# Turned context stored by the attention and read back by the feature stage, in place of a second turn

## The chip, the core and the metric

One core of a Trainium2 chip runs the whole program in one launch. TensorE (PE) multiplies, with its weight loads shown as PEld; VectorE (DVE), ScalarE (ACT) and GpSimd (POOL) do the elementwise work; SyncE (SP) issues most transfers, POOL some. The metric is the device time of the launch in microseconds, lower is better.

## The reference, cut to what matters

Four layers run one after another on x, 16 batches of 128 rows by 512 features: attention over a context, a ternary linear layer, an attention between features, and a mixture of 16 experts. The change concerns what the first and third layers share, the context `ctx` (16 x 128 x 512):

```python
k = (memory_tokens @ wk.T); v = (memory_tokens @ wv.T)            # first layer, memory_tokens = ctx

def _L1_xattn_ref(Q, K, V):                                       # third layer, K = V = ctx
    x = jnp.einsum('bdn,bdm->bnm', Q, K) / sqrt(dk)
    score = jax.nn.sigmoid(x)
    return jnp.einsum('bvn,bnm->bvm', V, score)

x = x + jnp.tanh(g_xattn[1]) * _L1_xattn_ref(_layernorm(x, axis=-1), ctx_2048, ctx_2048)
```

For each batch the third layer forms a 512 x 512 table of scores and multiplies the context by it.

## The kernel before, in words

All matrix products keep single precision by splitting each operand into a high part (rounded by a copy to the fp32r type) and a low part (the rest), and by three matmuls: high by high, high by low, low by high. `mm3` (lines 45 to 49) issues them, so every product shows as L47, L48 and L49.

The first two layers and the third lie in `attention_and_ternary`. The order of work is written out by hand: strings of words such as `cT.2 q.1.2` are turned by `steps` into one list, `plan`, and each engine walks that list and issues its own part of every step. The strings are `start`, `first_group`, `group` (twice) and `last_group`, for four groups of four batches; behind them a loop over `m` from 0 to 63 writes the feature stage's order, four values of `m` per batch. `between` mixes in what is left of the ternary layer and the first steps of what follows.

**Attention.** Step `cT.b` turns a batch's context: PE transposes four 128 x 128 pieces into a PSUM bank (L502), ACT copies the high part into `cT`, DVE subtracts to get the low part. `cT` holds four batches (two pairs), each reused by the batch four later. The key and value products read it.

**Feature stage.** Per batch b: SP loads the context again, unturned, into one of four places (`cx.b`, L387). POOL splits it into high and low for the scores (`ks.b`: L449, L451, and L453 for the low part of the normed x; tiles of `Wk`). ACT makes the normed x and its high part (`an`, L713; `qh`, L721). PE makes four score products (`aS`, output SC). ACT takes the sigmoid twice (`ag`, L726 and L729), DVE subtracts for the low part (L869, tile `Wq`). PE makes four value products into one bank M (`ap` three times, then `aO`), whose left operand is the turned context `avT`, in the tile of `Wv`. DVE adds the result to X and takes its statistics (L874, L877).

The turned context comes from step `aT.b`: PE transposes the loaded context as in attention (L502, tile T), ACT copies the high part (L660) and DVE subtracts (L881). `avT` has two places. `aT.0` and `aT.1` stand at the end of `last_group`; `aT.{b+1}` stands before the third value product of batch b. The step also makes SP wait before it loads the batch four later into the same place:

```python
if n == 2 and 1 <= b + 1 < NB and b:
    text += [f"aT.{b + 1}"]
...
sp.wait_ge(t_fill, at(T_KINDS, ("aT", b - GB)))
sp.wait_ge(aq_lo, b - GB + 1)
```

`wait` and `wait_ge` hold an engine until a counter is reached; everything behind on that engine stands still too.

Of the kernel before, what the change touches and what calls it, by code (L numbers as in the profile page):

```python
# [114 lines left out]
def attention_and_ternary(nc, c, x, g_x, g_f, fw, fb, ctx_in, mask, norm_w, wq, wk, wv, wo, wg, sw1, sw2, sw3):  # L115

    X, identF = c["X"], c["identF"]
    with ExitStack() as st:
# [3 lines left out]
        def sem(name):  # L122
            return st.enter_context(nc.semaphore(name))
# [49 lines left out]
        avT = flat(W["v"][:, :, :, :])[:, 0:4 * D].rearrange("p (b h d) -> p b h d", b=2, h=2)  # L173
# [22 lines left out]
        TILED = ("xT", "cT", "v", "g", "S", "rc", "bc", "pv", "oT", "oP", "st", "sf", "sx", "nm", "mk", "u", "uT", "fm")  # L196

        def steps(text, g):
# [31 lines left out]
        start = ("W.k Wh.k Wl.k mf cT.0 cT.1 gt W.q Wh.q Wl.q sx.0 sx.1 sx.2 sx.3 xa.0 k.0.0 k.0.1 W.v Wh.v Wl.v.0.1 xb.0 Wl.v.2.3 "  # L230
# [33 lines left out]
        for m in range(MS):  # L264
# [8 lines left out]
            if n == 2 and 1 <= b + 1 < NB and b:  # L273
                text += [f"aT.{b + 1}"]
# [3 lines left out]
            if n == KC - 1 and b + GB < NB:  # L278
                text += [f"cx.{b + GB}"]
# [5 lines left out]
        SPLIT, T_KINDS = ("xT", "cT", "aT", "rT"), ("xT", "cT", "aT", "rT", "pT", "bc", "uT", "ft")  # L285
# [34 lines left out]
        ac_in = [sem(f"ac_in{n}") for n in range(GB)]  # L320
# [18 lines left out]
        with nc.Block() as block:  # L339
            @block.sync  # L340
            def _(sp):
# [35 lines left out]
                for s in plan:  # L377
                    if s[0] == "cx":
# [3 lines left out]
                        elif b < GB:  # L382
                            sp.wait_ge(s_fill, 4 * (NB - 2))
                        else:
                            sp.wait_ge(t_fill, at(T_KINDS, ("aT", b - GB)))
                            sp.wait_ge(aq_lo, b - GB + 1)
                        sp.dma_start(aCX[b % GB], ctx_in[b]).then_inc(ac_in[b % GB], 16)  # L387
                    elif s[0] == "rn":
# [22 lines left out]
            def _(pool):  # L411
# [20 lines left out]
                for s in plan:  # L432
# [5 lines left out]
                    elif kind == "tb":  # L438
# [3 lines left out]
                            .then_inc(a_powered, 1)  # L442
                    elif kind == "ks":
# [32 lines left out]
            def _(pe):  # L476
# [11 lines left out]
                def transposes(s, tf):  # L488
# [9 lines left out]
                    else:  # L498
                        src = {"rT": lambda k: rows[:, t, k * P:(k + 1) * P], "aT": lambda k: aCX[t % GB][:, k * P:(k + 1) * P], "xT": lambda k: xn[:, t % 2, k * P:(k + 1) * P], "cT": lambda k: CT[:, t % 2, k * P:(k + 1) * P],
# [33 lines left out]
                for s in plan:  # L533
# [8 lines left out]
                    elif kind in T_KINDS:  # L542
# [7 lines left out]
                        elif kind == "aT":  # L550
                            pe.wait_ge(ac_in[t % GB], 16 * (t // GB + 1))
# [22 lines left out]
                    elif kind in ("ap", "aO"):  # L574
                        n = s[2] if kind == "ap" else KC - 1
                        m, mf = KC * t + n, at(M_KINDS, ("aO", t))
                        if n == 0:
                            wait(pe, m_act, up_to(M_KINDS, BY_ACT, mf - 2))
                            wait(pe, m_dve, up_to(M_KINDS, BY_DVE, mf - 2))
                            pe.wait_ge(t_lo, at(SPLIT, ("aT", t)))  # L580
# [1470 lines left out]
```

## Time and profile before

| What | Value |
|---|---|
| Median of 3 runs | 1234.98 us (1234.42 to 1236.65) |
| The profiled execution | 1236.93 us |
| Its span in the trace | 1235.2 us, so 1.73 us lie around it |
| PE busy | 1162.0 us, 94% of the span |
| DVE, ACT, POOL busy | 685.9, 579.1 and 438.0 us |
| Granted TensorE clock, mean | 0.989 of full speed |
| First value product to the last update of X | 377.1 to 492.7 us |

The profile gives each engine's busy time, the time it sat idle and the instruction that ended each idle stretch. A busy PE is not PE at its peak, since matmuls overlap; where they run back to back, the distance between two starts is the price of one.
### The profile page before, as it was taken

What the parts mean: (1) busy time and instruction counts of PE and PEld (TensorE: products, weight loads), DVE (VectorE), ACT (ScalarE), POOL (GpSimd) and SP (SyncE); (2) the same over time, 40 slices, a digit from 0 to 9 for tenths busy, and PEclk for the clock granted to TensorE, in tenths of its full rate; (3) what the DMA queues carried; (4) which work ended last, traced back from release to release, by engine and by line L of the source; (5) the groups of instructions that cost most, each with busy time, mean ns of one, the idle gap of its engine ahead of it and who ended that gap; (6) DMA issues with size and microseconds to landing.
All of it is one profiled execution on the core that took longest, in us unless ns stands there. A gap on an engine that the chain in (4) does not pass through costs nothing. (4 is left out here: it accounts for less than half of the span.)

```text
span 1235.2 us, 24835 instructions
## 1 busy us (share of the span) xinstructions
PE 1162.0 (94%) x7376; PEld 995.7 (81%) x7388; DVE 685.9 (56%) x1411; ACT 579.1 (47%) x1389; POOL 438.0 (35%) x530
## 2 busy tenths in 40 slices
PE   6999999999998898799999998999999999999995
PEld 6887888887876676577777877899999989998995
DVE  6776756666559999435766545432244452424241
ACT  5665645656578697631111115433344453434342
POOL 1103212213337663100047622444444435444443
PEclk9999999999999999899999999999999999999998
DMA  9110000000001210220002316664456574646464
GB/s 334 53 38 1 19 4 18 19 21 12 25 1 36 96 44 31 91 96 1 1 1 72 138 52 206 153 152 76 77 138 145 147 208 85 142 81 144 79 142 72
DMA packets 54332, 100.31 MB, mean 81 GB/s; under 512 B 5094, under 2 KB 21990, under 8 KB 54262
## 3 DMA queue, kind: packets, MB, share of 16 engines
q0 software_dynamic: 15824, 37.76, 16.0%
q1 hardware_dynamic: 38438, 61.65, 15.1%
q8 instruction: 40, 0.66, 0.2%
q14 instruction: 30, 0.25, 0.1%
HBM read 72.91 MB, written 26.48 MB: 80 GB/s over the span
## 5 line engine op out<-in xcount | busy, mean ns | idle before, releaser
L1901 PE MATMUL t_H<-m_W,t_xT 128*128 128x352 f32 x1632 | 281.9, 328 | 6.8 <-DVE m_W L1979 5.3
L1901 PEld LDWEIGHTS t_H<-m_W,t_xT 128*128 128x128 f32 x1632 | 263.2, 189 | 10.0 <-DVE m_W L1979 7.7
L1869 POOL DMA_INDIRECT out_dram<-t_ys,t_sid x68 | 109.6, 1612 | 223.8 <-ACT t_ys L1930 117.4
L738 ACT ACTIVATE pr<-SC,neg 128x128 f32<-128x128 f32 x256 | 90.7, 377 | 57.5 <-DVE neg L948 56.2
L1946 ACT ACTIVATE t_sl<-t_H 128x352 f32<-128x352 f32 x68 | 31.6, 465 | 175.3 <-PE t_H L1901 175.3
L2024 DVE TENSOR_TENSOR t_hT<-t_TH,t_hT 128x384 fp32r<-128x384 f32 x68 | 37.8, 556 | 101.8 <-ACT t_hT L1967 100.7
L2000 DVE TENSOR_TENSOR t_h<-t_H,t_sl 128x352 f32<-128x352 f32 x68 | 35.6, 524 | 105.0 <-ACT t_sl L1946 105.0
L47 PE MATMUL t_Y<-m_W,t_hT 128*128 128x512 f32 (+1 forms) x207 | 88.0, 425 | 4.8 <-issue 3.0
L1930 ACT ACTIVATE t_ys<-t_Y,t_wcol 128x512 f32<-128x512 f32 x69 | 47.4, 687 | 94.6 <-PE t_Y L49 94.6
L49 PE MATMUL t_Y<-m_W,t_hT 128*128 128x512 f32 (+1 forms) x207 | 82.2, 397 | 0.0
L48 PE MATMUL t_Y<-m_W,t_hT 128*128 128x512 f32 (+1 forms) x207 | 81.9, 396 | 0.0
L1214 POOL TENSOR_SCALAR m_W<-m_W,bst 128x128 fp32r<-128x128 f32 x64 | 49.6, 793 | 31.6 <-PE eL L1329 31.4
L869 DVE TENSOR_TENSOR Wq<-kT,Wq 128x512 fp32r<-128x512 f32 x64 | 56.2, 903 | 6.7 <-ACT Wq L729 6.6
L1410 ACT ACTIVATE ehT<-eh 128x512 fp32r<-128x512 f32 (+1 forms) x24 | 15.2, 632 | 91.8 <-DVE eh L1696 91.8
L738 ACT ACTIVATION_READ_ACCUMULATOR pr<-SC,neg 128x1 f32 x256 | 54.9, 215 | 0.0
L945 DVE TENSOR_REDUCE mx<-SC 128x4 f32<-128x512 f32 x64 | 43.8, 685 | 18.4 <-PE SC L629 18.2
L1860 POOL COPY t_sid<-m_vals 128x1 uint32 x68 | 52.8, 776 | 0.5 <-issue 0.5
L465 POOL TENSOR_TENSOR X<-X,upd 128x512 f32<-128x512 f32 x16 | 21.3, 1330 | 88.0 <-DVE upd L929 88.0
L1861 POOL COPY m_pos<-m_rowid 128x1 uint32 x68 | 51.6, 759 | 0.0
L47 PEld LDWEIGHTS t_Y<-m_W,t_hT 128*128 128x128 f32 (+1 forms) x207 | 39.4, 190 | 13.5 <-issue 5.8
L1020 POOL DMA_INDIRECT m_first<-rows_d,m_pos x36 | 37.3, 1035 | 35.0 <-POOL m_pos L1861 26.6
L1975 DVE TENSOR_TENSOR t_xT<-t_TX,t_xT 128x512 fp32r<-128x512 f32 x69 | 47.7, 691 | 3.2 <-ACT t_xT L1923 0.3
(454 smaller groups left out, 3135.5 us busy)
## 6 DMA issues: line engine op xcount, KB each, us to landing
m_raw<-in_L_ffn_w_dram SPq DMA_DIRECT2D x28, 704.0 KB, 5.8
m_raw<-in_L_ffn_w_dram SPq DMA_DIRECT2D x14, 512.0 KB, 6.9
CT<-in_ctx_dram SPq DMA_DIRECT2D x8, 512.0 KB, 3.8
X<-in_x_dram SPq DMA_DIRECT2D x4, 1024.0 KB, 13.3
rows_d<-rows_first SPq DMA_DIRECT2D x16, 256.0 KB, 2.0
out_dram<-X SPq DMA_DIRECT2D x3, 1024.0 KB, 4.3
m_raw<-in_L_ffn_w_dram SPq DMA_DIRECT2D x14, 192.0 KB, 6.7
CT<-in_ctx_dram SPq DMA_DIRECT2D x8, 256.0 KB, 2.7
```

Of the source, the lines that this page charges most:

```text
L47: pe.matmul(out, lhs(0), rhs(0), start=first, stop=False)
L48: pe.matmul(out, lhs(0), rhs(1), start=False, stop=False)
L49: return pe.matmul(out, lhs(1), rhs(0), start=False, stop=last)
L738: i = act.activation(pr[:, t % 2, slot, :], SC[t % HQ][:, slot * S:(slot + 1) * S], ACT.Exp, scale=SCALE0, bias=neg[:, t % 2, slot:slot + ...
L869: dve.tensor_tensor(as_[:, n, 1, :], asg[:, n, :], as_[:, n, 0, :].bitcast(F32), ALU.subtract).then_inc(as_lo, 1)
L1214: i = pool.tensor_scalar(tab_a[t % SLOTS][:, k, :], iP.bitcast(F32), place_p[:, t, k:k + 1], None, ALU.is_equal)
L1860: pool.tensor_copy(sid[:, b:b + 1], m["target"][:, bass.ds(n, 1)]).then_inc(zeroed, 1)
L1861: pool.tensor_copy(gid[:, b:b + 1], rowid[:, bass.ds(n + UT, 1)]).then_inc(zeroed, 1)
L1869: pool.indirect_dma_start(out=m["out_rows"][:, :], out_offset=bass.IndirectOffsetOnAxis(ap=sid[:, b:b + 1], axis=0), in_=ys[:, b, :], in_o ...
L1901: x_ = pe.matmul(bk[b % 2][:, 0:I], xT[:, b % 2, jx, k, :], W13[:, jw, k, j, :], start=k == 0 and jx == jw, stop=k == KC - 1 and jx == 1)
L1930: act.activation(ys[:, (b - 1) % UT, :], Y[(b - 1) % 2][:, :], ACT.Copy, scale=wcol[:, (b - 1) % UT:(b - 1) % UT + 1]).then_inc(y_evac, 1)
L1975: dve.tensor_tensor(xT[:, b % 2, 1, :, :], TX[:, :].rearrange("p (k t) -> p k t", k=KC), xT[:, b % 2, 0, :, :].bitcast(F32), ALU.subtract) ...
```

## The change

The attention's turned context, high and low, is stored to a scratch tensor in DRAM, `av_d`, in 16 new steps `sv.b` on SP, each behind the low part of `cT.b`. The feature stage reads it back in 16 new steps `al.b`, issued by POOL, into four places of `avT`. The 16 steps `aT.b` go, on PE, ACT and DVE.

```diff
-        avT = flat(W["v"][:, :, :, :])[:, 0:4 * D].rearrange("p (b h d) -> p b h d", b=2, h=2)
+        avT = flat(W["v"][:, :, :, :]).rearrange("p (b h d) -> p b h d", b=GB, h=2)
+        av_d = nc.dram_tensor("av_d", [NB, P, 2, D], F32, kind="Internal").ap()
...
-            "pT.15 u.0 qh.1 aS.0.2 bc.3 pv.3 ks.1 oT.3 uT.0 aT.0 aT.1 ag.0.1 oP.3 u.1 fm.0 ")
+            "pT.15 u.0 qh.1 aS.0.2 bc.3 pv.3 ks.1 oT.3 al.0 al.1 al.2 al.3 uT.0 ag.0.1 oP.3 u.1 fm.0 ")
...
-            if n == 2 and 1 <= b + 1 < NB and b:
-                text += [f"aT.{b + 1}"]
...
             if n == KC - 1 and b + GB < NB:
-                text += [f"cx.{b + GB}"]
+                text += [f"cx.{b + GB} al.{b + GB}"]
...
                         else:
-                            sp.wait_ge(t_fill, at(T_KINDS, ("aT", b - GB)))
                             sp.wait_ge(aq_lo, b - GB + 1)
...
+                    elif s[0] == "sv":
+                        b = s[1]
+                        sp.wait_ge(t_lo, at(SPLIT, ("cT", b)))
+                        sp.dma_start(av_d[b].rearrange("p h (k t) -> p h k t", k=KC), cT[:, b // 2 % 2, :, :, b % 2 * S:(b % 2 + 1) * S].bitcast(F32))\
+                            .then_inc(av_out[b % GB], 16)
...
+                    elif kind == "al":
+                        b = t
+                        pool.wait_ge(av_out[b % GB], 16 * (b // GB + 1))
+                        if b < GB:
+                            projected(pool, "v", NB - 1)
+                        else:
+                            summed(pool, KC * (b - GB) + KC - 1)
+                        pool.dma_start(avT[:, b % GB, :, :], av_d[b].bitcast(F32R)).then_inc(av_in[b % GB], 16)
...
-                            pe.wait_ge(t_lo, at(SPLIT, ("aT", t)))
+                            pe.wait_ge(av_in[t % GB], 16 * (t // GB + 1))
...
+                            if kind == "cT":
+                                wait(act, av_out[t % GB], 16 * (t // GB))
```

`summed(pool, KC * (b - GB) + KC - 1)` waits for the last value product of batch b - 4. The words `sv.2` to `sv.5` stand in each group some steps behind the `cT` of the same number, and `al.4` to `al.15` each at the end of batch b - 4's part of the loop. The last hunk makes ACT wait, before it overwrites a place of `cT`, until the store of the batch four earlier has landed. SP has 16 more transfers in the attention, each of 1024 pieces of 128 elements; POOL has 16, of 128 x 1024 elements.

DVE at the end of batch 1 in the feature stage, before (`Wq` is the scores' tile, `Wv` the turned context's, `M` the value product's bank, `bst` the statistics):

```order
L900 BN_STATS bst<-X 128x6
L869 TENSOR_TENSOR Wq<-kT,Wq 128x512 x2
L900 BN_STATS bst<-X 128x6
L869 TENSOR_TENSOR Wq<-kT,Wq 128x512
L881 TENSOR_TENSOR Wv<-T,Wv 128x512
L869 TENSOR_TENSOR Wq<-kT,Wq 128x512
L874 SCALAR_TENSOR_TENSOR X<-M,tg,X 128x512
L877 BN_STATS bst<-X 128x6
```

and the same place with the change:

```order
L900 BN_STATS bst<-X 128x6
L874 TENSOR_TENSOR Wq<-kT,Wq 128x512 x2
L900 BN_STATS bst<-X 128x6
L874 TENSOR_TENSOR Wq<-kT,Wq 128x512 x2
L879 SCALAR_TENSOR_TENSOR X<-M,tg,X 128x512
L882 BN_STATS bst<-X 128x6
```

The subtraction for the turned context has gone from between two of the scores' low parts; nothing else moved. PE and ACT lose their part of the step in the same way.

POOL from the second key split to the fourth, before (`Wk` holds the splits, `fbrow` and `upd` are what the ternary layer adds to X):

```order
L453 TENSOR_TENSOR Wk<-xn,Wk 128x512
L469 TENSOR_TENSOR X<-X,fbrow 128x512
L465 TENSOR_TENSOR X<-X,upd 128x512
L473 TENSOR_TENSOR X<-X,upd 128x512
L449 CAST Wk<-qT 128x512
L451 TENSOR_TENSOR Wk<-qT,Wk 128x512
L453 TENSOR_TENSOR Wk<-xn,Wk 128x512
L469 TENSOR_TENSOR X<-X,fbrow 128x512
L473 TENSOR_TENSOR X<-X,upd 128x512
L449 CAST Wk<-qT 128x512
```

and with the change:

```order
L464 TENSOR_TENSOR Wk<-xn,Wk 128x512
L453 DMA Wv<-av_d 128x1024 x4
L480 TENSOR_TENSOR X<-X,fbrow 128x512
L476 TENSOR_TENSOR X<-X,upd 128x512
L484 TENSOR_TENSOR X<-X,upd 128x512
L460 CAST Wk<-qT 128x512
L462 TENSOR_TENSOR Wk<-qT,Wk 128x512
L464 TENSOR_TENSOR Wk<-xn,Wk 128x512
L480 TENSOR_TENSOR X<-X,fbrow 128x512
L453 DMA Wv<-av_d 128x1024
L484 TENSOR_TENSOR X<-X,upd 128x512
L460 CAST Wk<-qT 128x512
```

Four transfers now stand behind the second key split and one ahead of the fourth; one more follows in each later batch, up to batch 11's.

## Rows read from the trace of the kernel before

**Rows 1.** Windows: engine busy times, granted clock, DMA share; attention, then the feature stage

```profile
60.00:340.00 280.00, 269.50 (x2412) 231.06 (x2419) 187.26 (x454) 161.80 (x593) 72.29 (x67) 1.00 0.06 17
...
377.00:400.00 23.00, 19.91 (x90) 14.56 (x88) 22.55 (x37) 18.16 (x35) 19.70 (x15) 1.00 0.09 24
400.00:440.00 40.00, 34.09 (x151) 26.26 (x154) 36.53 (x53) 28.32 (x54) 25.66 (x20) 0.96 0.27 86
440.00:493.00 53.00, 47.94 (x221) 37.40 (x219) 50.26 (x83) 44.96 (x85) 26.49 (x21) 1.00 0.09 27
```

**Rows 2.** Timeline of DVE: the update of X (L874) closing a batch

```profile
384.28 0.74 DVE L874 SCALAR_TENSOR_TENSOR X<-M,tg,X 128x512 f32<-128x512 f32 x1
...
448.50 0.75 DVE L874 SCALAR_TENSOR_TENSOR X<-M,tg,X 128x512 f32<-128x512 f32 x1
...
455.18 0.74 DVE L874 SCALAR_TENSOR_TENSOR X<-M,tg,X 128x512 f32<-128x512 f32 x1
...
492.66 0.75 DVE L874 SCALAR_TENSOR_TENSOR X<-M,tg,X 128x512 f32<-128x512 f32 x1 [0.47 <-PE M L49]
```

**Rows 3.** Waits of PE, 377 to 493 us

```profile
PE M L47 <- DVE Wq L869: 5.5, 4, 1.5
...
PE M L47 <- DVE Wv L881: 2.4, 2, 2.1
...
PE SC L47 <- POOL Wk L453: 1.1, 1, 1.1
```

**Rows 4.** Groups of instructions on DVE, 377 to 493 us: the context's low part

```profile
L881 DVE TENSOR_TENSOR Wv<-T,Wv 128x512 fp32r<-128x512 f32 x14 | 9.6, 682 | 0.8 <-ACT Wv L660 0.6
```

**Rows 5.** Timeline of PE: 15 matmuls between first two rows, then a turn's end

```profile
448.29 0.39 PE L47 MATMUL SC<-Wk 128*128 128x512 f32 x1
...
451.70 0.60 PE L502 MATMUL T<-identF,qT 128*128 128x128 f32 x4
452.06 0.48 PE L47 MATMUL M<-Wq,Wv 128*128 128x512 f32 x1
```

**Rows 6.** Timeline of DVE: low parts of scores (L869) and context (L881)

```profile
445.37 1.89 DVE L869 TENSOR_TENSOR Wq<-kT,Wq 128x512 fp32r<-128x512 f32 x3
...
449.95 4.10 DVE L869 TENSOR_TENSOR Wq<-kT,Wq 128x512 fp32r<-128x512 f32 x3
453.98 0.68 DVE L881 TENSOR_TENSOR Wv<-T,Wv 128x512 fp32r<-128x512 f32 x1
454.58 0.68 DVE L869 TENSOR_TENSOR Wq<-kT,Wq 128x512 fp32r<-128x512 f32 x1
```

**Rows 7.** Timelines of PE, DVE and POOL before the first value product

```profile
372.65 0.47 PE L47 MATMUL M<-Wo,oT 128*128 128x512 f32 x1 [0.60 <-DVE oT L963]
...
377.09 0.40 PE L47 MATMUL M<-Wq,Wv 128*128 128x512 f32 x1
...
370.89 1.62 DVE L963 TENSOR_TENSOR oT<-o,oT 128x512 fp32r<-128x512 f32 x1 [0.70 <-ACT oT L744]
...
370.69 1.27 POOL L469 TENSOR_TENSOR X<-X,fbrow 128x512 f32<-128x512 f32 x1
```

**Rows 8.** Timeline of POOL: first and last part of one key split

```profile
449.28 0.61 POOL L449 CAST Wk<-qT 128x512 fp32r<-128x512 f32 x1 [2.35 <-PE SC L49]
...
451.76 1.74 POOL L453 TENSOR_TENSOR Wk<-xn,Wk 128x512 fp32r<-128x512 f32 x1
```

**Rows 9.** POOL's transfers and the DVE burst beside one (min/median/max ns in the second)

```profile
744.25 0.83 POOL L1843 DMA_DIRECT2D out_dram<-X  x1 [8.98 <-POOLq L1146]
...
L1020 POOL DMA_INDIRECT m_first<-rows_d,m_pos x36: 972/1002/1646, 728.4 to 1209.4; - x36
...
962.04 1.65 POOL L1020 DMA_INDIRECT m_first<-rows_d,m_pos  x1 [0.80 <-POOL m_pos L1861]
...
961.91 3.30 DVE L1979 TENSOR_TENSOR m_W<-m_raw,m_W 128x704 fp32r<-128x704 f32 x4 [0.59 <-ACT m_W L1927]
```

**Rows 10.** Transfers: issues by name and size: us from issue to landing

```profile
out_dram<-X POOLq DMA_DIRECT2D x1, 1024.0 KB, 5.1
```

More of the change, by code:

```diff
@@ L195, in attention_and_ternary @@
         NU = NB * HQ
-        TILED = ("xT", "cT", "v", "g", "S", "rc", "bc", "pv", "oT", "oP", "st", "sf", "sx", "nm", "mk", "u", "uT", "fm")
+        TILED = ("xT", "cT", "v", "g", "S", "rc", "bc", "pv", "oT", "oP", "st", "sf", "sx", "nm", "mk", "u", "uT", "fm", "sv")
         def steps(text, g):
@@ L228, in attention_and_ternary @@
         NQ, FIRST = GB * HQ, 3
-        start = ("W.k Wh.k Wl.k mf cT.0 cT.1 gt W.q Wh.q Wl.q sx.0 sx.1 sx.2 sx.3 xa.0 k.0.0 k.0.1 W.v Wh.v Wl.v.0.1 xb.0 Wl.v.2.3 "
+        start = ("W.k Wh.k Wl.k mf cT.0 cT.1 sv.0 sv.1 gt W.q Wh.q Wl.q sx.0 sx.1 sx.2 sx.3 xa.0 k.0.0 k.0.1 W.v Wh.v Wl.v.0.1 xb.0 Wl.v.2.3 "
                  "k.0.2 k.0.3 xd.0 nm.0 nm.1 W.g Wh.g.0.1.2 Wl.g.0 xT.0 xT.1 Wh.g.3 Wl.g.1.2.3 mk.0 q.0.0 q.0.1 nm.2 nm.3 "
@@ L283, in attention_and_ternary @@
         scaled = [slice(0, GB), slice(GB, 2 * GB), slice(2 * GB, NB)] + [slice(2 * p, 2 * p + 2) for p in range(NB // 2)]
-        SPLIT, T_KINDS = ("xT", "cT", "aT", "rT"), ("xT", "cT", "aT", "rT", "pT", "bc", "uT", "ft")
+        SPLIT, T_KINDS = ("xT", "cT", "rT"), ("xT", "cT", "rT", "pT", "bc", "uT", "ft")
         BY_ACT, BY_DVE = ("q", "k", "g", "fg"), ("v", "pv", "oP", "fm", "aO")
@@ L319, in attention_and_ternary @@
         added, biased, q_step, f_step, some_ok = (sem(n) for n in ("added", "biased", "q_step", "f_step", "some_ok"))
-        ac_in = [sem(f"ac_in{n}") for n in range(GB)]
+        ac_in, av_out, av_in = ([sem(f"{w}{n}") for n in range(GB)] for w in ("ac_in", "av_out", "av_in"))
         a_norm, aq_hi, ak_hi, aq_lo, as_fill, as_hi, as_lo, as_used, a_scales, a_powered, a_seen, a_shift = (sem(n) for n in (
@@ L498, in transposes @@
                     else:
-                        src = {"rT": lambda k: rows[:, t, k * P:(k + 1) * P], "aT": lambda k: aCX[t % GB][:, k * P:(k + 1) * P], "xT": lambda k: xn[:, t % 2, k * P:(k + 1) * P], "cT": lambda k: CT[:, t % 2, k * P:(k + 1) * P],
+                        src = {"rT": lambda k: rows[:, t, k * P:(k + 1) * P], "xT": lambda k: xn[:, t % 2, k * P:(k + 1) * P], "cT": lambda k: CT[:, t % 2, k * P:(k + 1) * P],
                                "pT": lambda k: pr[:, t % 2, k, :], "uT": lambda k: u[:, k * P:(k + 1) * P]}[kind]
@@ L549, in _ @@
                             pe.wait_ge(row_ready, t + 1)
-                        elif kind == "aT":
-                            pe.wait_ge(ac_in[t % GB], 16 * (t // GB + 1))
                         elif kind == "cT":
@@ L579, in _ @@
                             wait(pe, m_dve, up_to(M_KINDS, BY_DVE, mf - 2))
-                            pe.wait_ge(t_lo, at(SPLIT, ("aT", t)))
+                            pe.wait_ge(av_in[t % GB], 16 * (t // GB + 1))
                         pe.wait_ge(as_lo, m + 1)
-                        i = mm3(pe, M[(mf - 1) % 2][:, :], lambda h: avT[:, t % 2, h, n * P:(n + 1) * P], lambda h: as_[:, n, h, :],
+                        i = mm3(pe, M[(mf - 1) % 2][:, :], lambda h: avT[:, t % GB, h, n * P:(n + 1) * P], lambda h: as_[:, n, h, :],
                                 n == 0, n == KC - 1)
@@ L654, in _ @@
                         act.wait_ge(t_fill, tf)
-                        if kind == "aT":
-                            if t < 2:
-                                projected(act, "v", NB - 1)
-                            else:
-                                summed(act, KC * (t - 2) + KC - 1)
-                            act.activation(avT[:, t % 2, 0, :], src, ACT.Copy).then_inc(t_hi, 1)
-                        elif kind == "rT":
+                        if kind == "rT":
                             projected(act, "g", NB - 1)
@@ L877, in _ @@
                         dve.bn_stats(c["bst"][:, t, :], X[:, t, :]).then_inc(a_seen, 1)
-                    elif kind == "aT":
-                        tf = at(T_KINDS, s)
-                        dve.wait_ge(t_hi, tf)
-                        dve.tensor_tensor(avT[:, t % 2, 1, :], T[(tf - 1) % 2][:, :], avT[:, t % 2, 0, :].bitcast(F32), ALU.subtract)\
-                            .then_inc(t_lo, 1)
                     elif kind == "rT":
```

16 rows, old and new, of tables (first_group, group, last_group) are left out of this document.

## The prediction, written before the changed kernel was run

> **What bounds the kernel now.** I read the windows first, to see which engine is full in which stage, then the distances between batches, then what PE waits for, and last the timelines of single instructions. The windows show the attention, where the stores would go, with PE busy 269.5 of 280 us and the transfers at 0.06 of their engines: PE bounds it and nothing else is near. In the feature stage it is another picture. DVE is busy 22.55 of 23 us, then 36.53 of 40, then 50.26 of 53, PE 19.91, 34.09 and 47.94 in the same windows [rows 1]. A batch ends with the update of X, L874. From the first to the sixteenth of these lie 108.4 us (384.28 to 492.66), 7.2 per batch; a quiet one in the middle takes 6.68 (448.50 to 455.18) [rows 2]. PE needs less. Fifteen matmuls lie between 448.29 and 451.70, 0.227 us each, and the next turn takes 0.36, from 451.70 to 452.06 [rows 5]; so 24 matmuls and a turn are 5.8 us. PE's waits point at DVE too: 5.5 us for the scores' low part, 2.4 for the turned context's low part, and only 1.1 for POOL [rows 3]. So the feature stage runs by DVE, with PE close behind.
>
> DVE is full partly because it waits while it counts as busy. Three low parts of the scores take 1.89 us when nothing disturbs them and 4.10 at 449.95, over POOL's key split, which fills 449.28 to 453.50 [rows 6, 8]. POOL's elementwise work thus counts double: what stands on it can hold DVE.
>
> **The change, part by part.**
>
> *The turn inside the stage.* Fourteen of the sixteen turns lie between 377 and 493 us [rows 4]. Where DVE is the chain, each gives back what L881 takes there: 0.60 us from its start to the next one's (453.98 to 454.58) [rows 6]. Where PE is the chain, it gives 0.36 [rows 5]. The bounds are 14 x 0.36 = 5.0 and 14 x 0.60 = 8.4 us. I take 0.50 each, 7.0 us: DVE is the fuller engine, but a quiet batch of 6.68 less 0.60 is already near the 5.5 that 24 matmuls need. The ACT copies that go cost nothing today: ACT is busy 44.96 of 53 us [rows 1], and the chain passes it only for the scores.
>
> *The two turns ahead of the stage.* Before the first value product PE waits 0.60 us for the low part of the attention's last output, L963, which starts at 370.89 and takes 1.62 because POOL's L469 runs from 370.69 to 371.96 [rows 7]. With the change POOL issues four transfers there instead. An undisturbed DVE subtraction of this size takes 0.68 [rows 6], so L963 ends 0.94 us earlier and PE starts as much earlier. Between 372.65 and 377.09 nothing else holds PE for long. I take 0.9; the bounds are 0 (the transfers hold DVE as L469 did) and 0.94.
>
> *The issues on POOL.* A transfer issued by POOL occupied it 0.83 us for 1 MB [rows 9]; these are of half that size, and I keep 0.83. The four at the front end near 374.0, ahead of anything waited for. Of the twelve others, one per batch, five (those ahead of the fourth, fifth, sixth, eighth and ninth key splits) fall where POOL works without pause, on key splits, additions of the ternary layer and powers: POOL is busy 19.70 of 23 us there, and PE waited 1.1 us for its split [rows 1, 3]. Behind such an issue stand that key split and the score products that need it. All five in full are 4.2 us, none of them 0; since PE waited for POOL just once there, I charge half, 2.1. The other seven find room. Five values of m lie between the release of a split and its use, 30 matmuls or 6.8 us less the last product's own 0.7, and the split takes 4.22 [rows 5, 8]; the transfer is released three matmuls earlier than the split. So a quiet batch has 6.1 - 4.2 + 0.7 = 2.6 us for an issue.
>
> *Landing.* The first value product started at 377.09 [rows 7] and would start near 376.2. The first transfer is issued at 370.7; a transfer of twice its size took 5.1 us to land [rows 10], so it is there by 375.8. The later ones have three batches. I set this at nothing; if the first had to share with the three behind it, 2 MB in all, it could land at 370.7 + 2 x 5.1 = 380.9, 4.7 us late.
>
> *The stores.* Sixteen of 512 KB under the attention, where the DMA share is 0.06 [rows 1]. SP waits for the low part of `cT.b`, and behind it stand only loads for later batches; the new ACT wait is for a store that was issued a group earlier. I set both at nothing. No row shows a store in such small pieces. The lower bound is 0; for the upper I let the time in which PE is idle there, 10.5 us of 280, grow by half, 5.2 us, an arbitrary but generous share.
>
> *SP's dropped wait* lets context loads start earlier; they had room already: 0.
>
> **The sum.** 7.0 + 0.9 - 2.1 = 5.8 us less. The profiled execution took 1236.93 (span 1235.2), so 1231.1 of its kind; the median of the runs is 1234.98, 1.95 below that execution, which puts the median after at **1229.2**. With the bounds, without a rival: 5.0 + 0 - 4.2 = 0.8 to 8.4 + 0.9 = 9.3 us less.
>
> **The rivals.** *Slower: POOL's issues wait for DVE.* POOL and DVE hold each other up in elementwise work, as shown, and DVE is nearly always busy with subtractions of two SBUF tiles. One row bears on whether a transfer's issue is held too: an indirect one took 1.65 us beside a burst of four such subtractions, where the median is 1.00, and the burst did not stretch (3.30 us for four) [rows 9]. So DVE would not lose, but an issue can. With that 0.65 it costs 1.48. If it had to sit out a burst of three low parts it would cost 0.83 + 1.89 = 2.7 [rows 6, 9]. Then the five issues in POOL's full stretches cost 13.6 and the seven others 0.1 each beyond their room, 14.3 in all against the 7.9 gained: 6.4 us slower, **1241.4**. It decides from 7.9 / 5 = 1.6 us per issue. The Trainium skill has a rule against such a change. "SBUF — State Buffer", section "SBUF: two separate sides", says that DVE in a two-port mode locks GpSimd out, so that it can't write the descriptors of its transfers, and that a 620 ns transfer took some 3100 ns beside such a copy. By that figure, as an estimate, each issue costs 3.1 us and the sum would be some 11 us slower. The one row that shows the pair has 0.65 on top, so the trace agrees in direction and not in size.
>
> *No change: each of the five issues costs 1.48 in full.* That is 7.4 against 7.9: **1234.5**. POOL's full windows speak for it, its single wait of 1.1 against it.
>
> *No change by a hidden cost of the transfers*: the first lands late, or stores hold the attention. 4.7 or 5.2 of the 5.8 go: about **1234.2**. The low DMA share speaks against it.
>
> *More.* DVE gives 0.60 every time, POOL's issues fit, and the gaps go after which the clock fell. The granted clock is 0.96 over 40 us [rows 1], some 1.6 us lost at the lower level; should it stay at 1.00, the gain is 8.4 + 0.9 + 1.6 = 10.9: **1224.1**.
>
> *That it doesn't do what it says* can be set aside: the order of instructions shows the turns gone and no other matmul added.
>
> **How the numbers follow.** Forecast 0.55; more 0.12; no change by POOL 0.13; by the transfers 0.11; slower 0.09. A measurement of this kernel can tell about 0.2% from no change, 2.5 us, so faster means below 1232.5 and slower above 1237.4. The forecast gives 0.53 to faster and 0.02 to same; more gives 0.12 to faster; the POOL case 0.03 and 0.10; the transfers' case 0.04 to faster, 0.06 to same and 0.01 to slower; the slow rival 0.09. Faster 0.72, same 0.18, slower 0.10. The forecast's own range is 1226.0 to 1232.5. The range for 8 in 10 runs from 1224.0, the "more" case, to 1236.5, above both cases without change, and leaves the slow rival out.
>
> **What would show it.** In the profile after: no L502 on CT or qT in the stage; 16 updates of X some 0.5 us closer on average, 7 us over 15 intervals; issues on POOL near 0.83 us; PE without waits for a transfer; the attention's span unchanged. L963 near 0.7 us. Wrong would be issues beyond 1.6 us, PE waiting for POOL's low part by more than 5 us in all, a wait at the first value product, or attention longer than before.

## The result and the profile after

| | Before | After |
|---|---|---|
| Median of 6 runs each | 1235.45 us | 1240.48 us |
| Lowest and highest | 1234.23, 1236.65 | 1238.73, 1244.40 |
| The profiled execution (span) | 1236.93 (1235.2) | 1239.09 (1237.2) |
| Mean granted clock | 0.989 | 0.982 |
| First value product of the feature stage to its last update of X | 115.57 us | 121.13 us |

The ratio is 1.0041, with an interval of 1.0027 to 1.0056: the changed kernel is slower by some 5 us, where 5.8 us less had been forecast. The time lies outside the range.

The two profiled executions are 2.2 us apart and the medians 5.0. That of before was 1.5 above its median, that of after 1.4 below. Inside the traces the stage grew by 5.6 us; it began 1.2 earlier, and some 2.4 us less lie between its end and the end of the span, in parts that the change doesn't touch. So one stage length of one execution has to be read with a microsecond or two of doubt, and the verdicts below go by the medians of many runs.

The windows of after, the attention first, answer to [rows 1]:

```profile
60.00:340.00 280.00, 270.17 (x2420) 231.20 (x2419) 187.15 (x453) 161.72 (x594) 72.27 (x67) 1.00 0.13 40
377.00:400.00 23.00, 18.93 (x81) 13.45 (x80) 22.66 (x35) 17.45 (x33) 20.37 (x17) 1.00 0.34 105
400.00:440.00 40.00, 31.83 (x125) 24.14 (x124) 33.45 (x44) 23.68 (x45) 25.26 (x24) 0.87 0.49 148
440.00:493.00 53.00, 46.33 (x183) 36.56 (x182) 45.69 (x71) 38.87 (x73) 30.58 (x27) 0.90 0.25 76
```

The attention carries its stores for nothing: PE 270.2 us busy of 280 against 269.5, the DMA share doubled to 0.13. Over the three windows of the feature stage together PE, DVE and ACT are less busy than before and only POOL is busier (76.2 us, 71.9 before), and yet the stage is longer. What got worse is the granted clock, 0.87 and 0.90 where 0.96 and 1.00 stood. That is no accident of one execution: the mean clock of the six runs of after is 0.979 to 0.984.

The new transfers, on the page of after, and in its timelines what they do ahead of the stage:

```profile
av_d<-cT SPq DMA_DIRECT2D x16, 512.0 KB, 3.5
Wv<-av_d POOLq DMA_DIRECT2D x16, 512.0 KB, 4.3
...
370.42 2.44 POOL L453 DMA_DIRECT2D Wv<-av_d  x4
...
370.64 0.69 DVE L963 TENSOR_TENSOR oT<-o,oT 128x512 fp32r<-128x512 f32 x1 [0.69 <-ACT oT L749]
```

L963 now takes 0.69 beside four issues, not 1.62 beside an addition [rows 7], and the first value product starts 1.17 us earlier, at 375.92. An issue takes 0.61 us, less than the 0.83 that was charged. No wait of PE is put down to a transfer.

What PE and the others wait for between 377 and 497 us (engine, line waited for: us in total, times, longest), where before PE's largest was 5.5 us [rows 3]:

```profile
ACT kT L731 <- PE SC L49: 29.8, 28, 5.8
POOL Wv L453 <- PE M L49: 19.7, 8, 7.5
...
PE M L47 <- DVE Wq L874: 12.0, 5, 3.9
...
DVE X L879 <- PE M L49: 7.7, 5, 2.5
```

and the wait of POOL in the kernel before:

```profile
POOL Wk L449 <- PE SC L49: 17.9, 8, 4.3
```

Three things differ. PE waits 12.0 us for the scores' low part. DVE waits 7.7 us for PE, at the update of X (the 0.47 us at the last one, [rows 2], is all of it before). And POOL stands 19.7 us at its own transfers, which may only be issued when PE has read the place they go to. It stood nearly as long before, 17.9 us, but at the key split, which needs PE's scores to be done. So POOL hardly waits longer; it waits earlier in its queue, ahead of work that needs nothing from PE.

**Where the time went: the third batch.** It is 10.80 us long (updates at 399.56 and 410.36) and was 8.30 before. PE in after:

```profile
401.80 0.39 PE L49 MATMUL SC<-Wk 128*128 128x512 f32 x1
406.11 0.79 PE L47 MATMUL M<-Wq,Wv 128*128 128x512 f32 x1 [3.92 <-DVE Wq L874]
406.70 0.63 PE L48 MATMUL M<-Wq,Wv 128*128 128x512 f32 x1
...
410.97 0.46 PE L49 MATMUL SC<-Wk 128*128 128x512 f32 x1
411.27 0.39 PE L47 MATMUL M<-Wq,Wv 128*128 128x512 f32 x1
```

and DVE beside it:

```profile
399.56 0.74 DVE L879 SCALAR_TENSOR_TENSOR X<-M,tg,X 128x512 f32<-128x512 f32 x1
...
400.95 1.20 DVE L785 TENSOR_TENSOR rstd<-tmp 128x2 f32<-128x2 f32 x1
...
404.97 0.49 DVE L820 TENSOR_SCALAR fu<-fu,fsc 128x512 f32<-128x512 f32 x1
405.37 2.49 DVE L874 TENSOR_TENSOR Wq<-kT,Wq 128x512 fp32r<-128x512 f32 x4
410.36 0.75 DVE L879 SCALAR_TENSOR_TENSOR X<-M,tg,X 128x512 f32<-128x512 f32 x1 [2.50 <-PE M L49]
```

From 399.56 to 405.4 DVE has a block of work of its own, the update, its statistics and the ternary layer's quantisation, and makes no low part. PE runs dry at 402.2 and stands 3.92 us. When DVE is through, its four low parts take 2.49 us and PE has all it needs, but ten matmuls take 0.63 us each with their starts 0.43 apart, not 0.227 [rows 5]: the lower clock level. That is 10 x 0.2 = 2.0 us, and DVE, done at 407.86, waits 2.50 for PE before the update. The same place before, PE and in the last row DVE:

```profile
400.99 0.47 PE L47 MATMUL M<-Wq,Wv 128*128 128x512 f32 x1 [2.09 <-DVE Wv L881]
...
404.62 0.63 PE L48 MATMUL SC<-Wk 128*128 128x512 f32 x1
405.05 0.52 PE L49 MATMUL SC<-Wk 128*128 128x512 f32 x1
405.40 0.60 PE L502 MATMUL T<-identF,CT 128*128 128x128 f32 x4
407.14 0.50 PE L47 MATMUL M<-Wq,Wv 128*128 128x512 f32 x1 [1.14 <-DVE Wq L869]
...
402.64 0.54 DVE L780 TENSOR_TENSOR rstd<-tmp 128x2 f32<-128x2 f32 x1
```

Before, too, the clock fell once (seven slow matmuls, 402.06 to 404.62), but under DVE's block, where PE would have waited anyway; then came a turn, work for which PE needs nothing that DVE is late with, and the wait left was 1.14 us. The slow phase cost nothing there; its 7 x 0.2 = 1.4 us went into the wait. The run b3 below shows this. Its feature stage is the one of before, turns and all, but its clock stayed up at that place:

```profile
404.51 0.60 PE L523 MATMUL T<-identF,CT 128*128 128x128 f32 x4
407.88 0.79 PE L47 MATMUL M<-Wq,Wv 128*128 128x512 f32 x1 [2.77 <-DVE Wq L892]
...
411.67 0.75 DVE L897 SCALAR_TENSOR_TENSOR X<-M,tg,X 128x512 f32<-128x512 f32 x1 [1.45 <-PE M L49]
```

PE did the same turn, then stood 2.77 us; five slow matmuls followed, DVE waited 1.45 us for PE, and the batch took 9.71 us. So 1.4 of the 2.5 us by which the third batch grew come and go without the change. Against b3 the gap is 1.15 us wider. 0.36 of it is the turn. Most of the rest is DVE's block, 5.8 us long where it was 5.15: L785 takes 1.20 us where L780, the same step, took 0.54. Each of the two ends with an instruction of POOL's key split (at 402.14 in after, at 403.16 in before).

Before has that one phase of slow matmuls in the stage. After has five: from 406.70 (10 matmuls), 421.66 (7), 448.98 (7), 469.17 (7) and 483.56 (6), each behind one of PE's five widest gaps there (3.92, 2.49, 2.12, 2.29 and 2.26). Behind its four shorter gaps, 0.88 to 1.76, there is none. By batch, the distance between updates of X, after less before:

```
batch        1     2     3*    4     5*    6     7     8*    9*   10    11*   12*   13*   14    15
before     7.82  9.15  8.30  9.08  8.32  7.44  7.19  6.92  6.68  5.98  7.12  6.67  6.99  6.06  4.66
after      7.84  8.52 10.80  9.55  9.53  7.15  5.99  7.92  6.51  5.99  8.12  7.35  8.36  5.44  4.78
difference  .02  -.63  2.50   .47  1.21  -.29 -1.20  1.00  -.17   .01  1.00   .68  1.37  -.62   .12
```

In the seven with a star at least two slow matmuls of after start (a phase can reach into the next batch): together they are 7.6 us longer. The eight others are 2.1 us shorter. So the turn's removal does pay where the clock stays up, though less than was forecast. What the starred ones lose is more than three times as much, but not by the clock alone: the wider gap ahead of each phase is in them too. The 37 slow matmuls are 7.4 us of PE's time, an estimate at 0.2 us each; the runs below say how much of it reached the total.

### The profile page after: what moved, and what is told of

It reads as the page before. It is cut to its first block and busy times, and to the rows that moved or that the text cites. A ratio compares the mean times of both kernels' runs of the same rounds, so it can differ in the third digit from the quotient of the medians.

```text
span 1237.2 us, 24702 instructions
## 1 busy us (share of the span) xinstructions
PE 1162.0 (94%) x7323; PEld 994.5 (80%) x7324; DVE 681.2 (55%) x1395; ACT 571.8 (46%) x1373; POOL 446.2 (36%) x546
## 5 line engine op out<-in xcount | busy, mean ns | idle before, releaser
L743 ACT ACTIVATE pr<-SC,neg 128x128 f32<-128x128 f32 x256 | 90.6, 376 | 57.5 <-DVE neg L948 56.1
L874 DVE TENSOR_TENSOR Wq<-kT,Wq 128x512 fp32r<-128x512 f32 x64 | 61.1, 993 | 9.2 <-ACT Wq L734 9.0
L731 ACT ACTIVATE kT<-SC 128x512 f32<-128x512 f32 x64 | 38.7, 605 | 30.7 <-PE SC L49 30.7
```

The costliest lines, as they stand in the source:

```text
L743: i = act.activation(pr[:, t % 2, slot, :], SC[t % HQ][:, slot * S:(slot + 1) * S], ACT.Exp, scale=SCALE0, bias=neg[:, t % 2, slot:slot + ...
L874: dve.tensor_tensor(as_[:, n, 1, :], asg[:, n, :], as_[:, n, 0, :].bitcast(F32), ALU.subtract).then_inc(as_lo, 1)
```

## The experiments

Theories: **A**, the turns were work that PE did while DVE was in a block; without them PE's gaps are wider, the clock falls behind them, and slow matmuls come when PE is the late engine. **B**, POOL's transfers cost the time. **C**, the stores do. **D**, DVE's freed time is spent again under POOL's elementwise work. Twelve kernels were run. The texts written before the runs use A, B and D in this way (B in a1 takes in DVE being held by POOL); their "theory C", in a3 and a4, is another one: the clock is a bystander and the stage is set by DVE. "Stage" is always the time from the first value product to the last update of X in the profile of one execution. The same stage took 115.57 us in before and 116.95 in b3, so a difference under 1.4 us says nothing. Ratios are to the kernel before on the same chip, with a 95% interval, and "clock" is the median of the runs' mean granted clock, 0.982 in after and 0.987 or 0.988 in before on the chips of these runs.

**a1: the turn's PE part alone put back.** Into after, where each of the fourteen turns stood, four transposes of the identity that nobody reads:

```diff
+            if n == 2 and 1 <= b + 1 < NB and b:
+                text += [f"dT.{b + 1}"]
...
+                        for k in range(4):
+                            pe.transpose(T[0][:, k % KC * P:(k % KC + 1) * P], identF[:, :], identF[:, :])
```

> The changed kernel with four transposes of the identity put back on PE where each of the fourteen turns stood in the feature stage; nobody reads them, and ACT's and DVE's parts of the turn stay away. Theory A (the turn was work that PE did while DVE was in a long block; without it the gaps are wider, TensorE's granted clock falls behind them, and the slow matmuls then come when PE is the late engine): fewer of the five phases of slow matmuls, 3 to 8 us less than the changed kernel, so 1232 to 1237. Theory B (the transfers issued by POOL, or DVE held by POOL, cost the time): PE gets more to do, so no less than the changed kernel, 1240 to 1243.

Measured: 1235.85 us, ratio 1.0013 (1.0000 to 1.0026), stage 117.86. Work that computes nothing makes the changed kernel 3 to 4 us faster. The third and the last window:

```profile
400.00:440.00 40.00, 33.20 (x144) 25.49 (x144) 33.19 (x45) 23.92 (x46) 25.44 (x24) 0.91 0.48 149
440.00:493.00 53.00, 48.05 (x226) 38.76 (x225) 48.15 (x75) 41.18 (x79) 29.82 (x27) 1.00 0.25 75
```

Two phases of slow matmuls are left of five, none behind 425 us, and the clock there is 1.00 again. The clock of the runs rose from 0.982 to 0.9865. This is A, and by the ratios (1.0041 and 1.0013) it is 3.5 of the loss of 5.1 us. One other effect is in it: the transposes also shift what lies beside what, and DVE's low parts come to 57.5 us where they were 59.2 in after (rows below).

**b2: only PE work taken from before.** The turns of the feature stage transpose one of four pieces, so three quarters of the turned context there are wrong; ACT and DVE do all they did:

```diff
-                        for k in range(KC):
+                        for k in range(1 if kind == "aT" else KC):
```

> The kernel before with one transposed piece of four in each of the sixteen turns of the feature stage (three quarters of the turned context stay what the bank held before); ACT's and DVE's parts of the turn are whole and there are no new transfers. PE has 0.27 us less to do per turn. Theory A: slower than before or equal, by 0 to 5 us, with more phases of slow matmuls than the one of before. Theory B: equal or up to 2 us faster.

The total, 1263.9 us, can't be used: other values reach the router, and the experts have 1728 matmuls where there were 1632. The stage can: 118.57 us, 3.0 longer than before's and 1.6 longer than b3's, by taking work away. b3 is the fairer partner, since neither has a slow phase at the first gap. Timeline of PE:

```profile
405.37 0.27 PE L502 MATMUL T<-identF,CT 128*128 128x128 f32 x1
408.74 0.79 PE L47 MATMUL M<-Wq,Wv 128*128 128x512 f32 x1 [3.09 <-DVE Wq L869]
409.33 0.63 PE L48 MATMUL M<-Wq,Wv 128*128 128x512 f32 x1
```

The gap of 1.14 has become 3.09, and twelve slow matmuls follow; but with the turns whole b3 has 2.77 and five there. Seven more come from 425.10, behind a gap of 2.32 us. At that place before and b3 have gaps of 1.99 and 1.98 with no slow matmul behind them, and the batch takes 8.32 us in both, 9.54 in b2. That is the mechanism of A in the kernel before, with neither transfers nor a changed DVE. Its size there is 1.6 us, hardly more than the scatter of a stage.

**a3 and b4: PE's gaps filled.** Identity transposes ahead of those value products that wait for a block of DVE, 122 in after, 72 in before:

```diff
+            fill = {11: 12, 13: 30, 20: 20, 24: 12, 33: 16, 45: 16, 53: 16}
+            if m in fill:
+                text += [f"dT.{m}.{fill[m]}"]
```

(`{13: 10, 20: 16, 24: 12, 33: 10, 45: 12, 53: 12}` in before.)

> The changed kernel with PE's gaps filled where its trace has them: 12, 30, 20, 12, 16, 16 and 16 transposes of the identity ahead of value products 11, 13, 20, 24, 33, 45 and 53, each about as long as the gap there, read by nobody. Theory A (the granted clock falls behind PE's gaps and its slow matmuls come when PE is late): no phase of slow matmuls in the stage, the stage 5 us or more shorter than in the changed kernel, and 1230 to 1235 in all. Theory C (the clock is a bystander; the stage is set by DVE and by what holds it): phases may go, the time stays within 2 us of the changed kernel.

> The kernel before with its own gaps filled (10, 16, 12, 10, 12 and 12 transposes of the identity ahead of value products 13, 20, 24, 33, 45 and 53). Theory A: within 2 us of before, since it has one phase of slow matmuls, and that beside a block of DVE. If filling pays by itself, 3 us or more less.

Measured: a3 1232.99 us, 0.9975 (0.9962 to 0.9989), stage 114.12; b4 1232.95, 0.9977 (0.9963 to 0.9991), stage 115.41. The windows of a3:

```profile
400.00:440.00 40.00, 37.74 (x197) 30.00 (x198) 36.69 (x48) 26.53 (x51) 29.50 (x25) 1.00 0.51 154
440.00:493.00 53.00, 50.48 (x242) 39.83 (x240) 48.22 (x77) 41.70 (x78) 28.41 (x26) 1.00 0.27 80
```

No slow phase is left in the stage of a3; b4 keeps one of four matmuls at 401.15. With the clock held, the change loses nothing against before with its own gaps filled, but it doesn't gain either: 1232.99 against 1232.95. So the clock is not all.

b4 gained 2.8 us by its ratio, more than the 2 that A allowed it and not quite the 3 of the other branch, and its stage is as long as before's. The clock of the runs fits the gain: 0.990 against 0.988, by an estimate 0.002 x 1235 = 2.5 us. So before loses to the clock as well, in some executions more than in the profiled one. Where in the program b4's gain lies is not shown.

**b1, b3 and a2: the transfers.** b1 gives before all 16 stores and 16 transfers back issued by POOL, into places nobody reads, with PE's wait for them; b3 the stores alone. a2 is after with the transfers back issued by SP:

```diff
+                        sp.dma_start(avT[:, b % GB, :, :].bitcast(F32), av_d[b]).then_inc(av_in[b % GB], 16)
...
-                        pool.dma_start(avT[:, b % GB, :, :], av_d[b].bitcast(F32R)).then_inc(av_in[b % GB], 16)
```

> The kernel before, turns and all, plus the sixteen stores and the sixteen transfers back, which land in places that nobody reads; PE waits for them as in the changed kernel. Theory A: within 2 us of the kernel before. Theory B: 4 to 6 us slower than the kernel before.

> The kernel before plus the sixteen stores alone; nothing is brought back. If the 1.7 us of the kernel with all transfers came from the stores under the attention: 1 to 2 us above before. If they came from POOL's transfers in the feature stage: equal to before within 1 us.

> The changed kernel with the sixteen transfers back issued by SP in place of POOL. Theory A: within 2 us of the changed kernel, since an issue takes POOL only 0.55 us; the five phases of slow matmuls stay. Theory B: the 5 us come back, near 1235.

Measured: b3 1235.62 us, 1.0002 (0.9988 to 1.0017), stage 116.95: C falls, at most 2 us of it could be left. b1 1236.5, 1.0018 (1.0005 to 1.0031), stage 116.97: 2 us more than b3, though the intervals overlap; that is at the edge of what A allowed (2) and under the 4 to 6 of B. a2 1237.08, 1.0017 (1.0006 to 1.0028), stage 117.68: 3 us faster than after, between what A (within 2) and B (5) had said. So B holds for 2 to 3 us, but not by the length of an issue. Timeline of POOL in after:

```profile
402.10 1.26 POOL L464 TENSOR_TENSOR Wk<-xn,Wk 128x512 fp32r<-128x512 f32 x1
410.85 0.55 POOL L453 DMA_DIRECT2D Wv<-av_d  x1 [7.49 <-PE M L49]
411.43 1.29 POOL L480 TENSOR_TENSOR X<-X,fbrow 128x512 f32<-128x512 f32 x1
412.65 0.62 POOL L460 CAST Wk<-qT 128x512 fp32r<-128x512 f32 x1
```

and of DVE there:

```profile
411.75 2.07 DVE L874 TENSOR_TENSOR Wq<-kT,Wq 128x512 fp32r<-128x512 f32 x1
414.21 1.32 DVE L874 TENSOR_TENSOR Wq<-kT,Wq 128x512 fp32r<-128x512 f32 x1 [0.39 <-ACT Wq L734]
```

The issue takes 0.55 us. But POOL stands 7.49 us for the last value product of the batch, and the ternary layer's addition (L480) is queued behind it, though it could have run long before. In a2, with no transfer on POOL's queue, the same addition and the same two low parts, and what POOL waits there for PE:

```profile
405.73 1.26 POOL L480 TENSOR_TENSOR X<-X,fbrow 128x512 f32<-128x512 f32 x1 [0.36 <-DVE fu L813]
...
413.37 0.67 DVE L874 TENSOR_TENSOR Wq<-kT,Wq 128x512 fp32r<-128x512 f32 x1
415.41 0.69 DVE L874 TENSOR_TENSOR Wq<-kT,Wq 128x512 fp32r<-128x512 f32 x1 [1.37 <-ACT Wq L734]
...
POOL Wk L460 <- PE SC L49: 21.6, 8, 5.8
```

The addition ran in POOL's idle time at 405.73, and the low parts take 0.67 and 0.69. In after it falls, with the key split pushed behind it, on DVE's low parts, which take 2.07 and 1.32. The wait itself costs nothing: POOL waits as long for PE in a2, 21.6 us, but at the key splits. What costs is the work that could have gone ahead. Batches 3 and 4 are 2.0 us shorter in a2 (9.81 and 8.52 against 10.80 and 9.55); a part of that is clock, since the third holds six slow matmuls there and nine in after. a2 still has four slow phases in the stage and a clock of 0.983, so it hardly touches A.

**a1 beside b1: what DVE's freed time is worth.** Both carry the transfers and PE's part of the turn. b1 also has ACT's copy and DVE's subtraction, 14 x 0.6 = 8.4 us of DVE. Yet it is only 0.65 us slower, 1.0018 against 1.0013, which the intervals don't tell from nothing, and its stage is no longer (116.97 against 117.86). Groups on DVE in the stage, a1 and then b1:

```profile
L882 DVE TENSOR_TENSOR Wq<-kT,Wq 128x512 fp32r<-128x512 f32 x62 | 57.5, 967 | 6.5 <-ACT Wq L742 6.4
```

```profile
L893 DVE TENSOR_TENSOR Wq<-kT,Wq 128x512 fp32r<-128x512 f32 x62 | 56.7, 940 | 2.7 <-ACT Wq L753 2.7
```

In a1 DVE's low parts are stretched by 0.8 us in all and it waits 3.8 us more for the sigmoid. From before to after the stretch is larger:

```profile
L869 DVE TENSOR_TENSOR Wq<-kT,Wq 128x512 fp32r<-128x512 f32 x62 | 54.8, 910 | 3.6 <-ACT Wq L729 3.6
```

```profile
L874 DVE TENSOR_TENSOR Wq<-kT,Wq 128x512 fp32r<-128x512 f32 x62 | 59.2, 994 | 5.3 <-ACT Wq L734 5.2
```

4.4 of the 8.4 us that DVE gave up stand again as longer low parts. L881 read one of its inputs from PSUM and took 0.675 to 0.692 us in all its 16 places in the trace; the low parts read two SBUF tiles.

**d1 and d2: POOL's hold on DVE made small.** In before and in after the two subtractions of the key split are cut to 8 of 512 columns, which leaves most low parts of keys and queries out:

```diff
-                        pool.tensor_tensor(ak[:, t % 2, 1, :], aCX[t % GB], ak[:, t % 2, 0, :].bitcast(F32), ALU.subtract)
+                        pool.tensor_tensor(ak[:, t % 2, 1, 0:8], aCX[t % GB][:, 0:8], ak[:, t % 2, 0, 0:8].bitcast(F32), ALU.subtract)
```

> The kernel before with POOL's two subtractions of each key split cut to 8 of 512 columns (the low parts of the context and of the normed x in the scores are left out but for these). Read by its feature stage, not by the whole time, since the scores change. Theory D (DVE's subtractions on two SBUF tiles stand still while POOL works on its own; so much of what the turn's removal gave DVE went into such standing): the mean of the scores' low part falls from 910 to some 700 ns and the stage, 115.6 us, gets 5 us or more shorter.

> The changed kernel with the same cut in POOL's subtractions. Theory D: the mean of the scores' low part falls from 994 to the same 700 ns as in the cut kernel before, and the stage is now shorter than there by 3 us or more, though it was 5.6 us longer with POOL's work whole. If the loss has nothing to do with POOL's work: the stage stays 3 us or more longer than in the cut kernel before.

Their totals, 1246.02 and 1242.73 us, hold 1728 expert matmuls each, so they can be compared with each other alone: 3.3 us less with the change. The stage is 104.17 us in d1 and 97.53 in d2. Updates of X on DVE (min/median/max ns, first and last start), d1 and then d2:

```profile
L874 DVE SCALAR_TENSOR_TENSOR X<-M,tg,X x16: 739/746/751, 385.6 to 482.3; 128x512 f32<-128x512 f32 x16
```

```profile
L879 DVE SCALAR_TENSOR_TENSOR X<-M,tg,X x16: 736/749/753, 387.1 to 477.5; 128x512 f32<-128x512 f32 x16
```

With POOL's hold small and no slow phase inside either stage, the change shortens it by 6.6 us (the 15 intervals between updates by 6.3): nearly the 7.0 forecast. In the middle a batch takes 5.93 in d1 and 5.44 in d2, 0.49 apart, where 0.50 had been taken for a turn. Of the 6.6 us the total shows half. A phase of twelve slow matmuls ahead of d2's stage, which starts 1.9 us later than d1's, takes a part of it in the profiled execution. The low parts' mean fell to 773 and 798 ns, not to the 700 expected; other POOL work still lies on some. POOL's transfers wait 22.7 us for PE in d2, but what is queued behind them is short. So POOL's work is what eats the turn's gain, by lying on DVE (D) and by being queued behind the waits (B); these two runs don't tell the one from the other, nor from the clock, which stayed up in both stages. For D by itself the stretched rows above and L785 speak. The Trainium skill, page "SBUF — State Buffer", section "SBUF: two separate sides", says that a DVE instruction with two SBUF inputs and a GpSimd one that reads SBUF shut each other out for a whole instruction. The traces agree: 0.67 free, 2.07 beside two POOL instructions.

**a4, b5 and c1: DVE's blocks cut.** If the gap comes from DVE's block, the block can be cut. The quantisation and the row statistics are each split in two steps, one value of `m` apart, so that low parts of the scores go between (`uh` and `ui` are the halves of `u`, `th` and `ti` of `ta`; the statistics at 44 and 52 likewise):

```diff
-        between = {2: "uT.-3", 3: "sf.-4", 4: "fm.-3 st.-2", 6: "st.-1", 8: "ra.-1 sf.-3", 10: "rb.-1", 12: "rd.-1 u.-2", 17: "uT.-2",
-                   18: "u.-1", 20: "fm.-2", 23: "uT.-1", 25: "sf.-2", 26: "fm.-1", 28: "sw", 30: "sf.-1", 32: "ta.1", 34: "tb.1", 36: "tc.1",
+        between = {2: "uT.-3", 3: "sf.-4", 4: "fm.-3 st.-2", 6: "st.-1", 8: "ra.-1 sf.-3", 10: "rb.-1", 12: "rd.-1 uh.-2", 13: "ui.-2", 17: "uT.-2",
+                   18: "uh.-1", 19: "ui.-1", 20: "fm.-2", 23: "uT.-1", 25: "sf.-2", 26: "fm.-1", 28: "sw", 30: "sf.-1", 32: "th.1", 33: "ti.1", 34: "tb.1", 36: "tc.1",
...
-                        scale_c(t)
+                        scale_c(t, second=kind == "ta")
...
-                        quantise(t)
+                        quantise(t, kind != "ui", kind != "uh")
```

a4 is after with it, b5 before with it, c1 after with it and with SP's issues.

> The changed kernel with DVE's long blocks in the feature stage cut in two: the quantisation and the row statistics run half ahead and half behind a low part of the scores. The same instructions, five of them one step later. Theory A: shorter gaps on PE, fewer phases of slow matmuls, 3 to 8 us less than the changed kernel. Theory C: less too, but by the gaps alone, 1 to 3 us. If neither holds (the gaps are set by POOL), no change.

> The kernel before with DVE's blocks cut in two, turns kept, no transfers. Theory A: before's gaps were filled in part by the turns, so it gains less than the changed kernel did, 0 to 4 us, 1231 to 1235. If it gains as much as the changed kernel did from the cut (10 us), the change costs its 5 us whatever DVE's blocks look like.

> The changed kernel with DVE's blocks cut in two and the transfers back issued by SP. Both helped alone (3.0 us by SP, 10 us by the cut, each against the changed kernel). If they add: 1228 to 1231; if the cut had already removed what the issues cost: 1231 to 1233.

Measured: a4 1231.80 us, 0.9960 (0.9944 to 0.9975), stage 113.92; b5 1233.30, 0.9974 (0.9959 to 0.9989), stage 114.00; c1 1232.66, 0.9972 (0.9963 to 0.9982), stage 112.42. The windows of a4:

```profile
400.00:440.00 40.00, 32.22 (x127) 24.02 (x127) 34.69 (x45) 24.32 (x47) 26.28 (x24) 0.91 0.49 151
440.00:493.00 53.00, 47.55 (x204) 35.74 (x202) 49.24 (x85) 43.26 (x81) 30.09 (x27) 1.00 0.29 85
```

Two short phases are left (five and six matmuls); behind 431 us PE's largest gap is 1.67 and the clock stays at 1.00. The split gives after about 10 us by the ratios and before 3. In after the clock rose from 0.982 to 0.987, by an estimate 6 us, and PE's wait for the low parts fell from 12.0 to 7.6 us in all; in before the clock stayed at 0.988, so those 3 us are shorter waits.

a4 has the lowest ratio of the study, 5 us under before, but its interval overlaps those of b5, c1, a3 and b4. So a gain over before is shown for the split and not for the change on top of it: with the split in both, after is at 0.9960 and before at 0.9974, their stages 113.92 and 114.00. SP's issues don't add their 3 us to the split either, which was the second branch of what c1 was run for: 0.9972 against 0.9960, intervals overlapping, though c1's stage is the shorter, 112.42. It had a slow phase ahead of the stage and two in it, the first of seven matmuls from 407.87, behind a gap of 2.84.

All of them side by side (phases of slow matmuls in the stage of the profile; totals of b2, d1 and d2 hold other expert work):

| Kernel | Ratio | Clock | Stage | Phases |
|---|---|---|---|---|
| before | 1 | 0.988 | 115.57 | 1 |
| after | 1.0041 | 0.982 | 121.13 | 5 |
| a1: after, turn's PE part | 1.0013 | 0.9865 | 117.86 | 2 |
| a2: after, SP issues | 1.0017 | 0.983 | 117.68 | 4 |
| a3: after, gaps filled | 0.9975 | 0.989 | 114.12 | 0 |
| a4: after, blocks cut | 0.9960 | 0.987 | 113.92 | 2 |
| c1: after, both of a2 and a4 | 0.9972 | 0.986 | 112.42 | 2 |
| b1: before, all transfers | 1.0018 | 0.988 | 116.97 | 1 |
| b3: before, stores | 1.0002 | 0.989 | 116.95 | 1 |
| b4: before, gaps filled | 0.9977 | 0.990 | 115.41 | 1 |
| b5: before, blocks cut | 0.9974 | 0.988 | 114.00 | 1 |
| b2: before, turns short | | 0.985 | 118.57 | 2 |
| d1: before, POOL short | | 0.9915 | 104.17 | 0 |
| d2: after, POOL short | | 0.9885 | 97.53 | 0 |

## Why the prediction was wrong, point by point

**The reading of what bounds** was half right. DVE was the fuller engine and PE close behind. But PE's place was read as room to spare; that its gaps have a consequence was left out.

**The turn inside the stage, 7.0 us less: this step failed.** It priced the turn by what it occupies, 0.36 on PE and 0.60 on DVE, and took both as pure loss to be got back. On PE the turn stood in the gaps and kept them shorter: putting PE's part back alone gave 3.5 us (a1), taking three quarters of it from before alone cost the stage 1.6 against b3 and 3.0 against before (b2). On DVE 4.4 of the 8.4 us went into low parts that stand under POOL. With the gaps filled in both kernels the change was worth nothing (a3 and b4: 1232.99 and 1232.95 us). Where POOL's work is short and the clock up, the step's size is right in the stage, 6.6 us (d1, d2), while the total shows 3.3. The forecast had a size that is there and missed its conditions.

**The clock** was in the text only as an upside, that "the gaps go after which the clock fell", 0.12. The sign was the other way: an engine that loses work and still waits for the same partner has wider gaps. Half of what was needed could be read before: the gap that ends at 400.99 is 2.09 us and is followed by slow matmuls, the one that ends at 407.14 is 1.14, right behind a turn, and is not. That the turn alone doesn't hold the clock up there took b3 to show.

**The start, 0.9 us less**, was right: 1.17 measured at the first value product, 1.08 at the first update, and L963 took 0.69, by the mechanism that was named. It holds for this execution; a slow phase ahead of the stage, which came in the profiles of six of the twelve other kernels, moves the start by more.

**The issues on POOL, 2.1 us more**, came to about the right sum by the wrong way. An issue takes 0.55 to 0.61 us, not 0.83, and never waits for DVE: the longest of the twelve in the stage took 0.61, with DVE busy 22.66 of 23 us beside some. So the slower rival, 2.7 us per issue, falls. The 3100 ns that the Trainium skill gives (page "SBUF — State Buffer", section "SBUF: two separate sides") are for a transfer beside a copy by DVE in a two-port mode. No issue here took anything like it, and whether an instruction of that kind ran beside one is not shown. What costs is what is queued behind the issue's wait for PE, an addition at 411.43 above all. The prediction had counted room for each issue and not asked what stands behind its wait. That the 2.1 us agree with the 2 to 3 measured is luck.

**The stores and the landing, 0**, were right as far as can be seen: b3 is at 1.0002 of before, give or take 0.0015, and PE never waited for a transfer.

**The chances and the signs.** Of the 0.10 for slower 0.09 went to one mechanism, the wrong one; a rival for gaps that grow wider was missing. That the time of this rival, 1241.4, lies 0.9 us from the measured 1240.48 is luck. And none of the four signs that were to show an error came: issues took 0.61 us at most, PE waited 1.7 us for POOL's low part, not at all at the first value product, and the attention's windows are alike. The signs covered POOL and the transfers, as the rivals did, and not PE's own gaps or its clock.

Settled by the runs: the loss is the clock behind wider gaps (a1 and a3, less clearly b2) and POOL's waiting transfers (a2, less clearly b1), with D as the reason why the freed DVE time doesn't pay for it. The parts don't add up by themselves, 3.5 us by a1 and 3.0 by a2 of 5.1, so they overlap. SP's dropped wait had no run of its own. Not settled is which gap makes the clock fall. One of 1.99 us in before (ended 419.48) had no slow matmul behind it, one of 1.99 in a2 (ended 448.26) had seven. And in a4 there is none behind one of 2.96:

```profile
405.45 0.50 PE L47 MATMUL M<-Wq,Wv 128*128 128x512 f32 x1 [2.96 <-DVE Wq L891]
```

## What to carry to other kernels

Before work is taken from an engine that waits in the same place anyway, ask what fills its gap afterwards: on TensorE a wider gap can cost in clock what the work was thought to cost, and cutting the partner's block, so that its gaps are shorter, was worth 10 us in the changed kernel and 3 in the one before. A transfer that has to wait for its place to come free belongs on a queue with nothing behind it that could run sooner, however short its issue is. And time freed on VectorE counts only as far as the instructions that move up don't come to stand under GpSimd.

## What the hardware showed that was not expected

Ten slow matmuls behind a gap of 3.92 us, six or seven behind gaps of 2.1 to 2.5 in after: at 0.2 us each such a fall costs PE 1 to 2 us. The fall isn't seen at the first matmul always: in a1 five run at full speed behind a gap of 3.50 before seven slow ones.

The same gap can go either way from one kernel to the next: seven slow matmuls behind the 2.09 us of before (ended 400.99), none behind 2.06 in b3 (ended 401.70). A phase near 373 us, ahead of the stage, is in the profiles of a2, a3, b2, c1, d1 and d2 and not in the others, and the stage starts between 375.92 us (after) and 379.98 (d2).

A transfer of 512 KB issued by POOL takes it 0.55 to 0.61 us and lands 4.3 us after (median); one in 1024 pieces of 512 bytes, issued by SP, lands in 3.5 us, sixteen of them beside the attention at no measurable cost.
